# First expert layer of a graph network: dense experts against sorted slots of one expert each, under a list schedule

## What is computed

```python
x = x + _L0_gnn_ref(_layernorm(x), src, dst, ...)          # table of 8 relations, gathered by edge, summed by node
x = x + _L0_ffn_ref(_layernorm(x), ...)                    # the experts below
x = x + _L1_gnn_ref(_layernorm(x), ...)                    # q, k, v, edge attention
x = x + _L1_ffn_ref(_layernorm(x), ...)

# _L0_ffn_ref: 6 experts of three 256x256 layers, the best 2 of 6 for each node
rh = relu(f @ router_w1 + router_b1)
top_w, top_i = top_k(softmax(rh @ router_w2 + router_b2), 2)
w = softmax(top_w)
h1 = relu(f @ expert_w1[e] + expert_b1[e]); h2 = relu(h1 @ expert_w2[e] + expert_b2[e]); y = h2 @ expert_w3[e] + expert_b3[e]
out = w[0] * y[top_i[0]] + w[1] * y[top_i[1]]
```

## Time and profile before

| | us |
|---|---|
| median of three runs | 1727.44 |
| lowest, highest run | 1724.54, 1735.62 |
| span of the profiled execution | 1668.6 |
| outside the span (median less span) | 58.8 |
| PE busy in the span | 1495.7 |
| POOL busy in the span | 781.2 |
| DVE busy in the span | 1028.6 |

### The profile page before, as it was taken

One profiled execution on the slowest core, in us unless ns is written; L12 is line 12 of the kernel. 1 busy time (PEld: TensorE's weight loads), 2 busy tenths in 40 slices (PEclk: granted clock), 3 DMA queues, 4 the chain that ended last, 5 costly groups with the idle time before them and its releaser, 6 DMA issues. The chain is left out here.

```text
span 1668.6 us, 23723 instructions
## 1 busy us (share of the span) xinstructions
PE 1495.7 (90%) x6795; PEld 1005.9 (60%) x6795; DVE 1028.6 (62%) x2542; ACT 615.6 (37%) x1534; POOL 781.2 (47%) x738
## 2 busy tenths in 40 slices
PE   4999788999999999998356799999999999999996
PEld 2554314665666777777233467767766767767785
DVE  6543244345445555545388789898898888896432
ACT  3121002333234343443022355554555445555341
POOL 1100277646755777600378666574746556540000
PEclk9999857999999999999556699999999999999997
DMA  8448456546766566631487885665757565641100
GB/s 258 164 161 261 142 151 172 154 115 191 213 175 180 166 190 178 164 94 47 137 252 216 267 253 165 193 180 167 208 152 212 143 196 169 179 122 39 29 7 9
DMA packets 191573, 270.07 MB, mean 162 GB/s; under 512 B 28295, under 2 KB 156035, under 8 KB 188867
## 3 DMA queue, kind: packets, MB, share of 16 engines
q1 hardware_dynamic: 148419, 144.77, 27.7%
q0 software_dynamic: 43008, 123.61, 26.8%
HBM read 196.22 MB, written 72.06 MB: 161 GB/s over the span
## 5 line engine op out<-in xcount | busy, mean ns | idle before, releaser
L1890 POOL DMA_INDIRECT att_kv<-table_kv,g_srcI x314 | 368.5, 1174 | 246.4 <-issue 180.4
L1149 POOL DMA_INDIRECT ex_hg<-table_h,z_idx x314 | 316.7, 1008 | 150.2 <-issue 84.9
L2441 PE MATMUL att_psR<-g_mw,att_h 128*128 128x256 f32 x640 | 163.9, 403 | 1.0 <-ACT att_h L2259 1.0
L2414 PE MATMUL att_psR<-att_t,g_mw 128*128 128x256 f32 (+1 forms) x640 | 154.8, 387 | 0.1
L1466 PE MATMUL ex_psG<-ex_hg,ex_oh 128*42 128x256 f32 x628 | 134.6, 427 | 13.3 <-DMA ex_hg<-table_h,z_idx 7.2
L751 PE MATMUL tab_psH<-e_u,tab_xT 128*128 128x512 f32 x320 | 142.6, 598 | 4.3 <-DVE e_u L532 4.3
L2441 PEld LDWEIGHTS att_psR<-g_mw,att_h 128*128 128x128 f32 x640 | 124.7, 200 | 23.0 <-ACT att_h L2259 4.0
L1387 ACT ACTIVATE ex_h<-ex_psH,g_cols 128x256 f32<-128x256 f32 (+1 forms) x240 | 97.3, 464 | 93.8 <-PE ex_psH L1488 93.1
L2414 PEld LDWEIGHTS att_psR<-att_t,g_mw 128*128 128x128 f32 x640 | 121.2, 199 | 16.6 <-issue 2.6
L1882 POOL DMA_DIRECT2D table_o<-att_part x59 | 54.2, 919 | 161.9 <-DMA table_o<-att_part 90.5
L2301 PE MATMUL att_psG<-att_kv,att_oh 128*42 128x264 f32 x628 | 109.5, 431 | 13.7 <-DVE att_kv L1997 13.3
(11 more groups left out here) (308 smaller groups left out, 2465.1 us busy)
## 6 DMA issues: line engine op xcount, KB each, us to landing
table_h<-tab_hs SPq DMA_DIRECT2D x20, 1024.0 KB, 4.0
att_eft<-in_eft SPq DMA_DIRECT2D x158, 64.0 KB
ex_db<-table_dst SPq DMA_DIRECT2D x79, 126.0 KB
table_ohT<-ex_ohT SPq DMA_DIRECT2D x79, 126.0 KB
att_ohT<-table_ohT SPq DMA_DIRECT2D x79, 126.0 KB
table_oh<-ex_oh SPq DMA_DIRECT2D x79, 84.0 KB, 2.3
att_oh<-table_oh SPq DMA_DIRECT2D x79, 84.0 KB, 4.0
table_kv<-ex_qkv SPq DMA_DIRECT2D x10, 512.0 KB, 4.8
```

The source lines that it names most:

```text
L1149: nc.gpsimd.indirect_dma_start(hg[:, t % RING0, :], None, d.h[:, :], bass.IndirectOffsetOnAxis(ap=g.idx0[:, t:t + 1], axis=0)).then_inc(go ...
L1890: nc.gpsimd.indirect_dma_start(kv[:, t % (RINGC * TP), H:H + 2 * D], None, d.kv[:, :], bass.IndirectOffsetOnAxis(ap=g.srcI[:, t:t + 1], ax ...
L2414: ins = nc.tensor.matmul(out[:, c * CB:c * CB + used(b)], g.mw1[:, e, k, c * P:(c + 1) * P], t3[:, k, 0:used(b)], start=(k == 0), stop=(k ...
L2441: ins = nc.tensor.matmul(out[:, q * D:(q + 1) * D], h1[:, n % 3, k, q * P:(q + 1) * P], g.mw2[:, e, k, :], start=(k == 0), stop=(k == DK - 1))
```

## The change

In blocks 0 to 8 the experts are no longer computed for every node. Block 9 stays dense.

- The nine blocks form four parts, (0, 1), (2, 3, 4), (5, 6) and (7, 8). For each block PE counts with triangular and all-one matrices (`rank`) which place each node has among those that chose the same expert, DVE turns that into row numbers (`pos`), and POOL scatters the block's normalised rows to the table `sorted_x` by indirect DMAs, two tiles times two choices: four a block (`scatter`).
- When a part's last block is counted, DVE works out a table of slots (`table`). A slot is 128 rows of one expert. There are 2 x tiles + 5 slots a part: 13, 17, 13 and 13, 56 in all, whatever the inputs. PE reads the expert numbers of a part into registers (`experts`).
- A slot is loaded by SP (`sL`), transposed by PE (`sX`, two transposes), and goes through three layers of two matmuls each (`sA`, `sB`, `sC`), whose weights are addressed by register; DVE copies each layer's sum out of PSUM, PE transposes it back (`tA`, `tB`) and ACT applies bias and relu. SP stores the output rows to `sorted_y` (`sS`).
- When all slots of a part are stored, POOL gathers the rows back by indirect DMAs, four a block (`fetch`), and DVE adds them with their weights (`combine`). The rest of a block is as before.
- `stage_tables` also stores zeros to `sorted_x` (8960 rows, 9.2 MB): three tiles of 128 KB with each of the tiles 2 to 18, and the remaining nineteen (2.4 MB) with the last tile.
- `order0` and its tables go. `plan0` is a list scheduler: it gives each piece the costs `COST0` ..., the dependences of `pieces0` and the ranks `RANK0`, and makes the order of all five engines, POOL's too. It also deals out five PSUM banks (`psR`), where before each kind of piece had its own.

```diff
+DENSE0, PARTS0 = (9,), ((0, 1), (2, 3, 4), (5, 6), (7, 8))
+CAP0 = [sum(B0[b] for b in part) * P for part in PARTS0]
+SLOTS0 = [2 * cap // P + E0 - 1 for cap in CAP0]
+AREAS = [max([E0 * cap + (E0 - 1) * P for cap in CAP0[j::2]] + [P]) for j in range(2)]
+SXROWS = sum(AREAS)
+XR, YR, DB = 4, 2, 3
...
+                    if tile >= 2:
+                        each = SXROWS // P // (NT - 2)
+                        n = each if tile < NT - 1 else SXROWS // P - (NT - 3) * each
+                        at = (tile - 2) * each * P
+                        sp.dma_start(d.sx[at:at + n * P, :].rearrange("(t p) c -> p t c", p=P),
+                                     zero[:, 0:D].unsqueeze(1).to_broadcast([P, n, D])).then_inc(cleared, 16)
...
-BEGIN0 = (8.50, 18.21, 26.73, 38.53, 45.39, 52.68, 59.85, 67.35, 74.08, 80.63)
-PACE0 = (12.94, 10.92, 15.34, 11.02, 11.48, 10.69, 10.69, 10.36, 10.73, 11.53)
...
+COST0 = {"gather": 4.1, "join": 0.95, "scatter": 4.2, "fetch": 4.2,
+         "group": 1.66, "turn": 0.62, "hidden": 1.05, "logits": 0.52, "rank": 0.35, "gateT": 0.38, "bias": 0.90,
+         "experts": 1.20, "sX": 0.31, "sA": 0.96, "tA": 0.31, "sB": 0.96, "tB": 0.31, "sC": 0.96, "A": 1.90, "B": 1.90, "C": 1.90, "turn2": 0.62, "q": 2.90}
...
+RANK0 = {"route": 5.8, "slots": 22.1, "pace": 1.0, "dense": -3.5, "post": 46.1, "fetch": 19.6}
...
+        add("POOL", "gather", i, 0, at, after("PE", "group", i - RING0 // TP))
...
+            add("POOL", "scatter", b, 0, at, after("DVE", "pos", b), after("DVE", "normed", b), again)
...
+            add("SP", "sL", n, p, at + RANK0["pace"] * j, prior("PE", "sX", XR), after("DVE", "table", p), *(after("POOL", "scatter", b, 0, LANDS) for b in part))
...
+            add("POOL", "fetch", b, 0, at + RANK0["fetch"], *(after("SP", "sS", m, p, LANDS) for m in range(AT0[p], AT0[p + 1])),
+                after("DVE", "combine", SPARSE0[n - 2] if n >= 2 else -1), after("DVE", "table", p))
...
+                def scatter(b):
+                    pool.wait_ge(s.pos_ready, sparse(b) + 1)
+                    pool.wait_ge(s.xn_ready, b + 1)
...
+                    for q in range(B0[b]):
+                        for j in range(2):
+                            nc.gpsimd.indirect_dma_start(d.sx[:, :], bass.IndirectOffsetOnAxis(ap=pos[:, T0[b] + q, j:j + 1], axis=0),
+                                                         xn[:, b % 2, q, :], None).then_inc(scattered[PART0[b]][b % 2], 16)
...
+                def fetch(b):
+                    pool.wait_ge(s.back_ready, PART0[b] + 1)
+                    for j in range(YR):
+                        pool.wait_ge(y_stored[j], count(AT0[PART0[b] + 1], YR, j))
...
+                for what, b, e in orders["POOL"]:
...
+                def turn_slot(what, n, p, src, made):
+                    out = take(what, n, p)
+                    for k in range(DK):
+                        ins = nc.tensor.transpose(out[:, k * P:(k + 1) * P], src[:, k * P:(k + 1) * P], g.ident[:, :])
+                    ins.then_inc(made, 1)
...
+                def layer_slot(what, n, p, x, w, made):
+                    out = take(what, n, p)
+                    for k in range(DK):
+                        ins = nc.tensor.matmul(out[:, 0:D], x[:, n % 2, k, :], w[:, ds(expert[n], 1), k, :].rearrange("p a c -> p (a c)"),
+                                               start=(k == 0), stop=(k == DK - 1))
+                    ins.then_inc(made, 1)
...
+                        if what == "sL":
...
+                            at = sp.value_load(tabR[0:1, b:b + 1], min_val=0, max_val=SXROWS - P)
+                            if b >= XR:
+                                sp.wait_ge(s.xs_made, b - XR + 1)
+                            sp.dma_start(xs[:, b % XR, :], d.sx[ds(at, P), :]).then_inc(x_got[b % XR], 16)
```

More of the change, by code:

```diff
@@ new lines, in plan0 @@
+def plan0(groups):
+    work = pieces0(groups)
+    left = {piece: len(deps) for piece, (_, _, deps) in work.items()}
+    follows = collections.defaultdict(list)
+    for piece, (_, _, deps) in work.items():
+        for dep, wait in deps:
+            follows[dep].append((piece, wait))
+    ready = {piece: 0.0 for piece in work}
+    open_, free = {e: [] for e in ("PE", "DVE", "ACT", "SP", "POOL")}, {e: 0.0 for e in ("PE", "DVE", "ACT", "SP", "POOL")}
+    for piece in work:
+        if not left[piece]:
+            open_[piece[0]].append(piece)
+    banks = [0.0] * 5
+    holder, freed_by = [None] * 5, {}
+    if groups:
+        banks[3] = banks[4] = float("inf")
+        holder[3] = holder[4] = ("nodes", 0, 0)
+    orders, bank, behind, last_q = {e: [] for e in free}, {}, {}, None
+    while any(open_.values()):
+        best = None
+        for engine, pieces in open_.items():
+            for piece in pieces:
+                start = max(free[engine], ready[piece])
+                if engine == "PE" and piece[1] in HELD0:
+                    start = max(start, min(banks))
+                if start < float("inf") and (best is None or (start, work[piece][1]) < best[0]):
+                    best = ((start, work[piece][1]), piece)
+        (start, _), piece = best
+        engine, what, b, e = piece
+        open_[engine].remove(piece)
+        end = free[engine] = start + work[piece][0]
+        orders[engine].append((what, b, e))
+        if engine == "PE" and what in HELD0:
+            n = min(range(5), key=lambda n: banks[n])
+            bank[what, b, e], behind[what, b, e] = n, holder[n]
+            holder[n], banks[n] = (what, b, e), float("inf")
+            by = HELD0[what]
+            freed_by[(by, what, b, e) if by in ("ACT", "DVE") else ("DVE", by, b, 0)] = n
+        if what == "q" and engine == "PE":
+            behind[what, b, e], last_q = last_q, (what, b, e)
+        if piece in freed_by:
+            banks[freed_by[piece]] = end + HOP
+        if engine == "DVE" and what == "prepare" and b == NSG // 2:
+            banks[3] = banks[4] = end + HOP
+        for other, wait in follows[piece]:
+            left[other] -= 1
+            ready[other] = max(ready[other], end + wait)
+            if not left[other]:
+                open_[other[0]].append(other)
+    assert sum(len(order) for order in orders.values()) == len(work)
+    return orders, bank, behind
@@ new lines, in _ @@
+                for what, b, e in orders["POOL"]:
+                    if what == "gather":
+                        if b * TP >= RING0:
+                            pool.wait_ge(s.summed, b - RING0 // TP + 1)
+                        for t in tiles(b):
+                            nc.gpsimd.indirect_dma_start(hg[:, t % RING0, :], None, d.h[:, :],
+                                                         bass.IndirectOffsetOnAxis(ap=g.idx0[:, t:t + 1], axis=0)).then_inc(got[t % RING0], 16)
+                    if what == "join":
+                        join(b)
+                    if what == "scatter":
+                        scatter(b)
+                    if what == "fetch":
+                        fetch(b)
@@ L1489, in layer @@
-                    ins.then_inc(s.half_made, 1)
+                            ins = nc.tensor.matmul(out[:, o * BLK0:o * BLK0 + w_], w[:, e, k, o * P:(o + 1) * P], x[:, k, 0:w_], start=(k == 0), stop=(k == DK - 1))
+                    ins.then_inc(s.a_made if what == "A" else s.b_made, 1)
                 def output(b, e):
-                    pe.wait_ge(s.half_ready, DK * half["B", b, e] + DK)
+                    pe.wait_ge(s.b_ready, halves_of(b, e))
+                    out = take("C", b, e)
```

735 lines of the change are left out of this document (559 added, 176 removed), and 5 rows, old and new, of the table BLOCK0.

## The result

The changed kernel takes 1878.7 us (median of four runs, 1864.8 to 1886.0) against 1726.8 for the kernel before: ratio 1.085, interval 1.079 to 1.091. It is 8.5% slower. The direction was forecast, the size was not: 1762, range 1712 to 1804.

The account below looks back on a forecast made before the run. PE set the pace, POOL close behind; POOL would take over. First slot of part (7, 8) at 721.3 + 104 + 7 + 9 = 841.3 against 806.9: span 1668.6 + 34.4 = 1703.0, plus 58.8 = 1761.8 us; range 1712 to 1804.

Parts of the forecast that it names:

- The basis of the sum: Whole kernel: profiled span 1668.6 us plus 34.4 gives 1703.0, plus 58.8 from span to median gives 1761.8 us.
- PE saves 94 us, dense out and slots in: PE in the expert stage: 280 us of dense experts go, 183 us of slots and about 3 of rank come.
- 72 indirect DMAs at 1.31 us in POOL's stream: POOL: 36 scatters and 36 fetches priced like gathers, 94 us in all, 52 of them ahead of the last gather.
- POOL up to the end of the last gather: 502 us: POOL's stream: 366 indirect DMAs at 1.31 us plus 25 joins at 0.9, setting the pace; last gather done at 702.4.
- In-order waits break it a little: 5 us, up to 15: Ahead of the last group: POOL waiting for slots and PE for copies disturb the cover, 5 us, up to 15.
- Behind the last group: End of the stage on PE: 104 us of work plus bubbles of 7 and 9 us, last matmul at 841.3.
- a wait of PE from the last group to the first slot of part (7, 8): PE between last gather and that slot: 13.9 us for join, scatter, landing and load; slot's transpose at 721.3.
- Rival 3, the falling clock: PE in the expert stage: a falling clock makes PE the pace again below 0.70; over 1804 us, chance 0.10.

Follow-up runs that it names:

- e8: Kernel before with 72 more indirect DMAs on POOL, one in each of groups 6 to 77, each gathering 128 unused rows: 1812.2 us, ratio 1.051.
- e13: Kernel before with 72 more indirect DMAs on POOL, one in each of groups 6 to 77, each of 16 rows: 1807.6 us, ratio 1.045.
- e14: Kernel before with 72 plain DMAs of 128 KB issued by POOL, one in each of groups 6 to 77: 1735.9 us, ratio 1.0035.
- e17: Changed kernel with its 72 indirect DMAs replaced by plain ones of the same size at the same places: 1828.8 us, ratio 1.056.
- e6: Changed kernel with the scatters of blocks 0 to 5 moved two gather groups later in POOL's order: 1875.5 us, ratio 1.087.
- e18: Changed kernel with its 72 indirect DMAs made plain, VectorE's halves ahead of the next preparation, scatters of blocks 0 to 5 two groups later: 1813.0 us, ratio 1.050.
- e1: Kernel before, unchanged, measured and profiled a second time: 1728.9 us, ratio 1.002, profiled span 1715.6 us.
- e9: Changed kernel with four more PE matmuls behind each of groups 14 to 49, 144 in all: 1877.3 us, ratio 1.090.
- e2: Changed kernel with a group's halves placed ahead of the next preparation on VectorE: 1875.3 us, ratio 1.084.
- e5: Changed kernel with slot layers taking weights of a constant expert in place of the register's: 1870.5 us, ratio 1.086.
- e16: Changed kernel with slot loads (from slot 4) and stores cut to 32 of 256 columns, fetches reading the node table: 1873.1 us, ratio 1.082.
- e7: Changed kernel with one indirect DMA for each scatter and fetch in place of four, 54 of 72 left out: 1832.2 us, ratio 1.060.

## Where the prediction was right, and where it failed

- **The basis of the sum** was off: one short execution stood for the kernel, and its 58.8 us to the median were treated as a constant. The changed kernel's profiled span (1878.4) lies 0.3 us from its median.
- **PE saves 94 us, dense out and slots in**: the count was right (672 slot rows), the price was not met (0.59 us a slot matmul, 0.54 even at a clock of 0.95, where I had 0.433). The saving is nowhere in the time.
- **72 indirect DMAs at 1.31 us in POOL's stream**: right as a row (0.95 and a gap of 0.30). The Trainium skill (DMA: Bandwidth & Descriptors, Latency and other measured facts) gives about 1 us of emission for a DMA from GpSimd. The rows of indirect DMAs here agree, 986 ns with 128 rows and 904 with 16 (e8, e13), and the plain one does not (612 ns, e14).
- **"POOL up to the end of the last gather: 502 us" is the step that failed.** It let the new DMAs fill the waits that POOL had in the earlier trace rows, and charged only what then stuck out. They do not fill them. The stream itself was priced well (rows and issue gaps of 481 us, where I had 502 without waits); what failed is that POOL would then hardly wait: it waited 150 us, and its last gather came at 828.0. By the time, 72 such DMAs cost 80 to 85 us in the kernel before (e8, e13), and making them plain gives back 50 in the changed one (e17). My sum left the end of the gathers at 702 where it was; the 52 DMAs ahead of it, at e8's 1.18 us, would have moved it by 61 us and the forecast to about 1823 (an estimate), still 56 us short of what was measured.
- **"In-order waits break it a little: 5 us, up to 15"**: the waits were far longer than that. POOL stood 57.7 us for positions alone, 51 of them ahead of the last gather. But taking most of that away gave nothing (e6), since it moved to the ring. With the indirect DMAs gone, both edits of order gave 16 us by the medians, not clear of noise (e18). What the term costs in time stays open between nothing and about what I gave it; no run shows it to be an explanation.
- **Behind the last group**: right in its sum, in part by luck. Its result was taken over at 863.6 and attention started 141 us later, against 97 us in e1 (751.8 to 848.4). My steps had 147 (841.3 + 10.7 for what follows, less a last group near 705). But 16 of my 147 were a wait of PE from the last group to the first slot of part (7, 8), and that slot's transpose began 1.7 us behind the hand-over (865.3), since the groups themselves ran 35 us behind the gathers. PE was then busy for 114 us where I had 104, and idle for 15 where I had 16. So a wait that did not come made up for work that I had priced too low.
- **Rival 3, the falling clock**: the clock did fall (0.72 and 0.76), to what the rival expected, and PE's work still was not the pace (e9). Its time above 1804 came, for another reason as far as e9 tells.
- **What stays open**: e18 is still 85 us over the kernel before. In its trace 42 us of this lie behind the last group (139 us there against 97), which leaves some 43 to 55 us ahead of it that no edit moved, neither alone (e2, e5, e6, e9, e16) nor in e18. So of the 112 us by which the changed kernel's last group is late against e1, plain DMAs in place of the indirect ones return 46 (863.6 to 817.9), and about half stays unexplained. Slots, ranks and positions with their many hand-overs are left as suspects; none of them was taken out by itself.

## What to carry to other kernels

Do not price work on a nearly full queue by what is left of its waits. If the waits come from a closed round with a short ring (four groups here), added transfers may come through whole: add the suspected operation to the old kernel first (e8 needed ten lines, and its 85 us would have turned a forecast of a small loss into one of a large one). And count indirect DMAs, not their rows or bytes: 1.1 to 1.2 us each on the time in the kernel before (e13, e8), 0.7 to 0.9 in the changed one (e17, e7), so 72 of them cost 50 us or more, against the 94 that PE was to be spared.

## What was not expected of the hardware

- An indirect DMA of 16 rows costs the kernel what one of 128 rows does (80 and 85 us for 72), and a plain DMA of 128 KB from the same queue a tenth of that (8 us).
- Hand-overs from PE to every waiting engine come up to 18 us late, and more of them with more indirect DMAs (sums of 0 to 40 us with 314 in the kernel before, 68 to 87 with 386 in it, 57 to 81 with 386 in the changed one).
- Where the clock falls at a late hand-over in e1, it falls behind it, not ahead of it. One ended at 338.3; stretches of 2 us round it (columns as above):

```profile
334.00:336.00 2.00, 2.00 (x11) 1.74 (x12) 0.00 (x0) 0.00 (x0) 1.39 (x3) 1.00 0.70 212
336.00:338.00 2.00, 0.29 (x3) 0.06 (x1) 0.00 (x0) 0.00 (x0) 0.59 (x1) 1.00 0.69 175
338.00:340.00 2.00, 0.54 (x3) 0.50 (x4) 1.54 (x5) 0.95 (x2) 1.12 (x2) 0.99 0.08 29
340.00:342.00 2.00, 2.00 (x8) 0.89 (x7) 0.43 (x2) 0.47 (x1) 1.69 (x2) 0.50 0.65 163
...
344.00:346.00 2.00, 2.00 (x11) 1.64 (x10) 0.42 (x1) 0.37 (x1) 1.19 (x2) 1.00 0.71 238
```

PE runs full at 2.4 GHz, stands idle for over 3 us, and goes on at 1.2 GHz for some 3 us. The same is seen behind the one that ended at 484.5 (0.50 from 488 to 490 us). At the one that ended at 460.8 PE had other work, busy for all of 456 to 462 us, and the clock stayed at 1.00. In the changed kernel late hand-overs are more frequent, and the mean clock is 0.72 at a busy share of 69%; in e1 it is 0.95 at 92%, in the earlier trace rows 1.00 at 98%.
